# Two-layer graph convolution with routed experts: three late dense chunks at the end of layer 1 for two, and 100 gathered groups in layer 2 for 104

## What is computed

```python
deg_out = segment_sum(edge_weight, src)
deg_in = segment_sum(edge_weight, dst)
norm = edge_weight * rsqrt(deg_out[src] * deg_in[dst] + EPS)
def layer(x, W, b):
    xt = x @ W
    agg = segment_sum(xt[src] * norm[:, None], dst)
    return relu(agg + b)
h6 = layer(layernorm(x), W6, b6)
h7 = layer(h6, W7, b7)
x = x + h7 @ Wp + bp
# then, over a layer norm of x: 8 experts with gelu, top 2 by router, weighted sum
x = x + experts(layernorm(x))
```

## Time and profile before

| what | value |
|---|---|
| runs | 3171.85, 3157.32, 3170.95 us |
| profiled execution | 3166.45 us |
| its span | 3164.5 us |
| TensorE's mean granted clock | 0.919 |
| busy: TensorE, VectorE, ScalarE, GpSimd | 83%, 60%, 27%, 62% |
| moved | 530.79 MB, 168 GB/s in the mean |

### The profile page before, as it was taken

The page is one execution under the profiler, slowest core; times in us unless marked ns, Lnnn a source line. Parts: engine busy times, 40 slices in busy tenths (PEclk is TensorE's granted clock), DMA queues, the critical chain, the costliest instruction groups (busy, mean ns, idle before and its releaser), DMA issues. The chain is left out here.

```text
span 3164.5 us, 53882 instructions
## 1 busy us (share of the span) xinstructions
PE 2631.7 (83%) x16919; PEld 2013.0 (64%) x16919; DVE 1911.0 (60%) x6028; ACT 861.5 (27%) x2052; POOL 1963.4 (62%) x1932
## 2 busy tenths in 40 slices
PE   4567479999999999995589988888888875899995
PEld 3456247676667776663466766666666553889984
DVE  9999878888888887864203545455545446522210
ACT  5677611122121222112201100000011001456652
POOL 0000277777777777777477777777777763467763
PEclk8699789999999999997899999899999885999997
DMA  4001355566665655668666766666666663344444
GB/s 129 0 22 43 115 166 181 201 204 203 199 203 193 195 188 191 203 199 276 207 201 226 259 213 213 194 217 215 226 220 221 219 226 93 60 66 71 70 67 115
DMA packets 197506, 530.79 MB, mean 168 GB/s; under 512 B 39338, under 2 KB 129247, under 8 KB 190463
## 3 DMA queue, kind: packets, MB, share of 16 engines
q0 software_dynamic: 102336, 252.47, 30.5%
q1 hardware_dynamic: 92174, 256.65, 22.4%
q10 hardware_dynamic: 2736, 18.48, 1.5%
HBM read 377.61 MB, written 156.24 MB: 169 GB/s over the span
## 5 line engine op out<-in xcount | busy, mean ns | idle before, releaser
L977 POOL DMA_INDIRECT arena<-table,src_i x1712 | 1673.7, 978 | 596.2 <-issue 514.5
L2098 PE MATMUL bank<-arena 128*128 128x257 f32 x4900 | 1246.5, 391 | 3.1 <-ACT zcd L1784 2.4
L2098 PEld LDWEIGHTS bank<-arena 128*128 128x128 f32 x4900 | 901.7, 194 | 202.5 <-issue 83.4
L2083 PE MATMUL bank<-arena 128*128 128x294 bf16 x2352 | 426.2, 295 | 49.6 <-DVE arena L1295 32.3
L1323 DVE TENSOR_TENSOR arena<-arena,bank 128x294 f32 x784 | 357.3, 456 | 176.4 <-PE bank L2083 164.9
L1295 DVE SCALAR_TENSOR_TENSOR arena<-iota_f,arena 128x256 f32<-128x256 f32 x784 | 366.8, 468 | 0.0
L2083 PEld LDWEIGHTS bank<-arena 128*128 128x128 bf16 x2352 | 226.4, 100 | 207.9 <-DVE arena L1323 46.3
L2111 PE MATMUL bank<-arena,s_all 128*32 128x257 f32 x3424 | 246.2, 408 | 75.1 <-DMA arena<-table,src_i 68.4
L1771 ACT COPY arena<-zero 128x2144 f32<-128x2144 f32 (+1 forms) x104 | 156.3, 1533 | 398.3 <-DMA chunks<-arena 335.9
L1003 POOL DMA_INDIRECT acc<-arena x105 | 178.7, 1702 | 126.6 <-ACT arena L1897 97.6
L1294 DVE TENSOR_SCALAR arena<-iota_key,arena 128x294 bf16<-128x294 bf16 x784 | 242.7, 310 | 0.0
(11 more groups left out here) (238 smaller groups left out, 2678.3 us busy)
## 6 DMA issues: line engine op xcount, KB each, us to landing
chunks<-arena SPq DMA_DIRECT2D x25, 3283.0 KB, 12.7
arena<-chunks SPq DMA_DIRECT2D x24, 3283.0 KB
arena<-table,src_i POOLq DMA_INDIRECT x1712
zsum<-zc SPq DMA_DIRECT2D x107, 128.5 KB, 3.2
zrow<-zsum SPq DMA_DIRECT2D x50, 257.0 KB, 4.7
arena<-in_W ACTq DMA_DIRECT2D x16, 512.0 KB, 16.9
rows_x<-arena SPq DMA_DIRECT2D x25, 264.0 KB
arena<-chunks ACTq DMA_DIRECT2D x2, 3283.0 KB
```

Of the source, the lines that this page charges most:

```text
L977: pool.indirect_dma_start(gat[:, r, j, 0:D], None, table[L], bass.IndirectOffsetOnAxis(ap=src_i[:, col:col + 1], axis=0)).then_inc(gathere ...
L2083: last = pe.matmul(ps_b[t % len(ps_b)], halves[:, t % OH_RING, word, :, half], ohk[:, t % OH_RING], start=(i == 0), stop=(i == 2))
L2098: last = pe.matmul(ps_ap, adj[:, c % 2, h, 0:P], xp[:, h], start=(h == 0), stop=(h == XB_ALL - 1))
```

## The change

`LATE_CT` becomes (31, 31, 18): three late chunks with 80 tiles instead of two with 48. Layer 2 then has 27 dense chunks, 816 tiles, and 100 gathered groups; layer 1 keeps its 24 chunks and 110 groups. `SHORT` becomes 16, so the first 16 chunks of layer 2 span 3 slots and the other 11 span 4, 92 slots. The pairs of layer 2's chunk part start at slots 10, 16, 19, 22, 26, 29, 34, 37, 40, 43, 49, 52, 57, 60, 65, 68, 73, 76, 81, 84 and 89, and the last four 4 slots earlier than before, at 92, 95, 100 and 103. The merged pair is pair 12, and `ROW_TILES` = 3 takes the place of `CT // 2` in `chunks_for`.

In the tail, turns 0 to 3 build 7, 8, 8 and 8 tiles (before 4, 5, 4, 5), turns 4 to 8 build 6, 6, 6, 6 and 7 (before 3, 4, 4, 4, 3), and turns 9 to 12 build 4, 5, 4 and 5 (before 4, 4, 4, 0). ScalarE issues the store of chunk 24 at turn 5 and of chunk 25 at turn 10, zeroes the buffer of chunk 26 at turn 8 and loads chunk 0 at turn 12. With an odd number of chunks the buffers of `adj` are exchanged in layer 2 (`(c + 1) % 2`). SyncE stores chunk 26 behind the table. The scratch area is resized (`SC_W`).

```diff
--- before.py
+++ after.py
@@ -32,7 +32,7 @@
 LONG_CHUNKS, LONG_CT = 16, 31
 CHUNKS, CT = 24, 30
 DT = LONG_CHUNKS * LONG_CT + (CHUNKS - LONG_CHUNKS) * CT
-LATE_CT, SHORT = (18, 30), 8
+LATE_CT, SHORT = (31, 31, 18), 16
 ALL = CHUNKS + len(LATE_CT)
 DTA = DT + sum(LATE_CT)
 N_CHUNKS = CHUNKS, ALL
@@ -44,7 +44,8 @@
 FIRST_GROUPS_AT = [5 * s + 18 for s in range(GPI)]
 COMBINE_AFTER = 3
 EARLY_PAIRS, LOOP_PAIRS, TAIL_FROM = 9, 22, 4
-MERGED_PAIRS = 11,
+MERGED_PAIRS = 12,
+ROW_TILES = 3
 ROOT_AT, SCALED_AT, TURNED_AT, RELU_AT, PROJECTED_AT, OUT_AT = 11, 12, 14, 16, 18, 20
 PAIR_SLOTS, PAIR_EVERY = 6, 3
 CAP = 6400
@@ -54,6 +55,8 @@
 PARTS_OUT = 16
 
 OFFS, CHUNK_OFFS = 16, 32
+
+L2_WORDS = 3640
 
 TINY_EW = 2.0 ** -15
 HUGE_EW = 2.0 ** 40
@@ -204,7 +207,7 @@
         XP_W = XB_ALL * ROW
         A_W = 2 * XB_ALL * AWID
         DTX = DTA
-        SC_W = 5 * DTX
+        SC_W = max(4 * DTX, 2 * DTX + E8, L2_WORDS)
         arena = sb("arena", [P, GAT_W + OHK_W + PART_W + CM_W + OHG_W + XP_W + A_W + SC_W])
         o_ohk = GAT_W
         o_part = o_ohk + OHK_W
@@ -571,12 +574,12 @@
             return L * GROUPS[0] + n
 
         FIRST_EXTRA = TAIL_FROM
-        EXTRAS = [range(DT + LATE_CT[0] * k // FIRST_EXTRA, DT + LATE_CT[0] * (k + 1) // FIRST_EXTRA)
-                  for k in range(FIRST_EXTRA)]
-        EXTRAS += [range(DT + LATE_CT[0] + LATE_CT[1] * k // 8, DT + LATE_CT[0] + LATE_CT[1] * (k + 1) // 8)
-                   for k in range(8)]
+        LATE_TURNS = FIRST_EXTRA, 5, 4
+        EXTRAS = [range(chunk_start(CHUNKS + i) + LATE_CT[i] * k // n, chunk_start(CHUNKS + i) + LATE_CT[i] * (k + 1) // n)
+                  for i, n in enumerate(LATE_TURNS) for k in range(n)]
         EXTRAS += [range(0)] * (TAIL - len(EXTRAS))
-        FIRST_STORED_AT, FIRST_LOADED_AT = FIRST_EXTRA + 1, FIRST_EXTRA + 3
+        STORED_AT = FIRST_EXTRA + 1, sum(LATE_TURNS[:2]) + 1
+        ZEROED_AT, FIRST_LOADED_AT = sum(LATE_TURNS[:2]) - 1, TAIL - 2
 
         def half_of(ap, g):
 
@@ -597,7 +600,7 @@
             return ceil_div(row * NG * TG, N)
 
         def chunks_for(b):
-            return next(c for c in range(ALL) if chunk_start(c) >= tiles_before((b + 1) * PT * P) + CT // 2)
+            return next(c for c in range(ALL) if chunk_start(c) >= tiles_before((b + 1) * PT * P) + ROW_TILES)
 
         def groups_for(L, b):
             return min(2 * ceil_div(tiles_before((b + 1) * PT * P) + 2 * TG - G0[L] * TG, 2 * TG), GROUPS[L])
@@ -767,7 +770,9 @@
 
             def load_chunk(c):
                 sp.wait_ge(applied[1], SLICES * (c - 1))
-                sp.dma_start(adj[:, c % 2].rearrange("p h w -> p (h w)"), chunks[c * P:(c + 1) * P, :]
+                if c >= CHUNKS:
+                    sp.wait_ge(chunk_stored, 16 * ALL)
+                sp.dma_start(adj[:, (c + 1) % 2].rearrange("p h w -> p (h w)"), chunks[c * P:(c + 1) * P, :]
                              ).then_inc(chunk_in[c % 2], 16)
 
             def load_pair(L, b, slot, turn, made):
@@ -879,6 +884,7 @@
                 load_l2_consts()
                 sp.wait_ge(p_stored, 16 * NPAIR)
                 carry_chunk(1, 0)
+                sp.wait_ge(chunk_stored, 16 * (ALL - 1))
                 store_chunk(ALL - 1)
 
                 def layer2_slot(n, c, j, g, stages):
@@ -1904,8 +1910,8 @@
                     block_out(j - 1, of[j - 1])
 
             def load_chunk(c):
-                act.wait_ge(chunk_stored, 16 * (CHUNKS + c + 1))
-                act.dma_start(adj[:, c].rearrange("p h w -> p (h w)"), chunks[c * P:(c + 1) * P, :]
+                act.wait_ge(chunk_stored, 16 * (CHUNKS + c + 2))
+                act.dma_start(adj[:, (c + 1) % 2].rearrange("p h w -> p (h w)"), chunks[c * P:(c + 1) * P, :]
                               ).then_inc(chunk_in[c], 16)
 
             def load_experts():
@@ -1994,10 +2000,15 @@
                     if k == FIRST_EXTRA:
                         zero_behind(CHUNKS - 1, 2)
                         zero_behind(CHUNKS - 1, 3)
-                    if k == FIRST_STORED_AT:
-                        act.wait_ge(added, DT + LATE_CT[0])
-                        act.dma_start(chunks[CHUNKS * P:(CHUNKS + 1) * P, :], adj[:, CHUNKS % 2].rearrange("p h w -> p (h w)")
+                    if k in STORED_AT:
+                        c = CHUNKS + STORED_AT.index(k)
+                        act.wait_ge(added, chunk_start(c + 1))
+                        act.dma_start(chunks[c * P:(c + 1) * P, :], adj[:, c % 2].rearrange("p h w -> p (h w)")
                                       ).then_inc(chunk_stored, 16)
+                    if k == ZEROED_AT:
+                        act.wait_ge(chunk_stored, 16 * (CHUNKS + 1))
+                        for i in range(SLICES):
+                            zero_chunk(ALL - 1, *slice_bounds(i))
                     if k == FIRST_LOADED_AT:
                         load_chunk(0)
                     tail_pairs(TAIL_PAIRS[k])
@@ -2095,7 +2106,7 @@
                 for h in range(first_of_step(step), first_of_step(step + 1)):
                     if h == XB_ALL - 1:
                         pe.wait_ge(chunk_carried, 16 * (L * CHUNKS + c + 1))
-                    last = pe.matmul(ps_ap, adj[:, c % 2, h, 0:P], xp[:, h], start=(h == 0), stop=(h == XB_ALL - 1))
+                    last = pe.matmul(ps_ap, adj[:, (c + L) % 2, h, 0:P], xp[:, h], start=(h == 0), stop=(h == XB_ALL - 1))
                 if step in ZERO_BEHIND:
                     last.then_inc(applied[L], 1)
 
```

## The result

The changed kernel takes 3230.89 us (median of 4 runs, 3220.93 to 3232.35), the kernel before on the same chip 3171.4 us. The ratio is 1.0188, with a 95% interval from 1.0149 to 1.0227: it is 1.9% slower, 60 us between the medians. The forecast was slower, but 3190 us with a range to 3214. The profiled execution took 3220.93 us, 54.5 us more than that of before (3166.45).

What follows compares the result with a forecast made beforehand. From slot 10 of layer 2 TensorE with the engines it talks to was taken as the bound, GpSimd closely behind. Tail +22 and layer 2 +2 gave +24 on 3166.45, so 3190 us, range 3154 to 3214.

Steps and rivals of the forecast that it cites:

- steps (a) to (d): Tail turns 0 to 8: added tiles +3, 0 and +8 us, chunk 0's load gone from turn 7, -9.
- (e): Tail, turn 10: ScalarE's store of chunk 25 amid pairs 19 to 22 stalls pair rows, +10 us, bounds +4 and +16.
- (g): Tail, turns 9 to 12: 6 more tiles, three of them always built ahead, +4 us, bounds +2 and +6.
- (h): Tail, turn 12: chunk 0's load delays the short transfers of the closing serial chain, +6 us, from nothing to 9.2.
- B: Layer 2's loop: GpSimd sets the pace, 32 fewer gathers save 41 us, whole 3147 us; chance 0.15.
- T2: Follow-up theory, layer 2: small transfers within 13 us behind a load are late; forecast four-slot part 440 to 450 us.
- Rival C: Tail and layer 2: transfers collide harder, tail +37, layer 2 +18 with waits unchanged, whole 3221 us; chance 0.16.
- Rival A: Tail: additions are hidden, only +4 us there, +2 in layer 2, whole 3172 us; chance 0.25.

Runs made afterwards that it cites:

- the last two runs: Four-slot chunk loads behind pair stores or in the second slot: changed kernel, chunk 0 behind the table, 3147.01 us; kernel before, group pairs 6 slots later, 3152.81 us.
- the last edit: Four-slot chunks whose first slot has no pair stores load in the second slot, against the changed kernel with loads behind stores and chunk 0 behind the table: ratio 0.9954.
- the fastest kernel: Changed kernel with chunk 0 loaded behind the table, four-slot chunk loads behind pair stores or, without such stores, in the second slot: 3147.01 us, ratio 0.9954.

## Why the prediction was right and wrong

**Right: the tail.** Turns 0 to 8, steps (a) to (d), were to give +2 and gave +2.8. VectorE's wait at turn 8 is gone, as forecast. Steps (e) and (g) with +14 gave +12.9: of it up to 7.9 is the store of chunk 25 (forecast +10), by the run that moves it. The two pairs' rows behind that store landed after 10.1 and 11.8 us, near the 10.8 of the earlier trace rows, but VectorE's wait for them, forecast at some 10 us, is only 4.7 there. Step (h) was forecast at +6 and the gap grew by 9.6; the load's part is 8.4 by the carried row (11.2 for 2.8), and the run with the load behind the table takes back 9.7. The means over all profiles that share each stage's code give +2.4, +10.1 and +7.4, together +20 for the +22, so the tail came out right, though no single step is settled to better than a few us.

**Right: the bound.** GpSimd did not set the pace, and B did not happen; its waits in the loop rose to 100 us. The three-slot part came out at 0.95 us idle a slot, as put.

**Wrong: the waits of the four-slot part.** The step that failed is the wait put on a four-slot slot. It reads "44 four-slot [...]: 36 + 60 = 96 for 112, -15". The 60 measured 82. The idle time is 36 + 82 = 118, +6 instead of -15, and the matmuls took 816.1 us for 794.2, +21.9 instead of +17.7, with the clock at 0.89 where they were dearer. I carried 1.37 us a slot over as if it were a property of such a slot. It is the result of which slots the pairs' small transfers fall in, relative to the chunk loads, and the change moved the group pairs by two slots against the dense ones. Moving them back takes 31 us off, with 66 us idle for the 60 of the forecast; giving the kernel before the new phase adds 61. With 31 us less in the loop, the changed kernel would have stood at 3200 us, inside the range; the run that does this alone has a ratio of 1.0102, and 1.0102 x 3171.4 is 3204.

**Rival C** came nearest with 3221. That the profiled execution took 3220.93 is luck: its tail of +37 measured +25, and its +18 in the loop measured +30. Its condition that the waits don't shrink held. Its mechanism was the right one, but it put the harder collisions into the wrong stage: the transfers collide harder, but in layer 2. **Rival A** asked for a first gather within 5 us of its old time; it came 27.4 us later. **Rival B** shows only where the collisions are gone: in the last two runs TensorE waits for gathers, 9.4 and 37.6 us.

The starts of the pairs were written in my account of the change. What I left out was to lay them beside the borders of the chunks, and to ask in which slot each pair's store stands behind a load. The wait of the earlier trace rows and that for `off_i` could have been given to single slots before the sum was made.

What stays open: with the shift the changed kernel's four-slot part is still 13 us above 44 slots at the old 10.24 us, and no run gives these to single slots. Why the last edit gained more than T2 had forecast is not followed up either. Why the run from ScalarE's queue one slot later is still slower than the changed kernel by 10 us in the four-slot part is not settled either.

## What to carry to other kernels

A wait per iteration read from a profile belongs to the arrangement that made it: when a change moves two periodic streams against each other, here pairs and chunk loads, write out the slots of both before and after, and give the measured waits to slots. In these runs a large transfer made late the small ones issued while it ran, in its own queue or another; so place it behind the last small transfer that somebody waits for and as far as possible ahead of the next, and judge a moved transfer by the next link of the chain, not by the wait that vanished. A landing time in the profile says little if the issuer itself was held until the large transfer was through.

## What the runs showed of the hardware

A 128.5 KB store on SyncE's queue beside a 3283 KB load on ScalarE's took 11.2 us to the read that waits for it (1547.50 to 1558.69), where the kernel before took 2.8 without such company. In the run with chunk loads on ScalarE's queue a store of the same size took 15.1 us (2429.96 to 2445.10). The Trainium skill (DMA: Bandwidth & Descriptors, Queues, rings and completion order) has each DMA engine take turns between its queues. With the load, the store and the gathers as three users of equal right, 2.8 us would become some 8.4 by that reading, an estimate. Both measured times are above it. With the 13.3 us that such loads take in the median, the first ends with the load (1545.39 + 13.3 = 1558.7) and the second 2 us behind it; no run here shows what happens inside the engines. The prediction's use of this rule, a stall of at most 9 for step (e), fits the 5 to 8 measured.

TensorE's granted clock, a mean of its two levels of 1.2 and 2.4 GHz in each stretch, was lower in the four-slot parts with more waiting. In that of the changed kernel it was 0.89 with 82 us idle of 494, in the run with its pairs moved back 0.93 with 66 of 464, in the fastest kernel 0.97 with 39 of 421. It does not follow the idle share step by step: the three-slot part had 0.97 with 8.2% idle in the changed kernel and 0.94 with 7.5% in the run with chunk 0 behind the table. The fastest kernel's four-slot part:

```profile
2137.00:2558.00 421.00, 381.91 (x2291) 287.94 (x2292) 235.27 (x1039) 44.74 (x120) 319.78 (x333) 0.97 0.68 221
```

The same matmuls took 412.1 and 381.9 us: 30 of the 73 us between the two windows are clock, and 43 are waits.
